# Normalising on GpSimd instead of VectorE, with a new order of the attention loop

## What is computed

```
x = x + attention(adapted_layernorm(x))      # adapter chosen by language, 16 heads of 16, one key and value head
x = x + ffn(cond2(x))                        # expert chosen per sequence, four more matrix layers
```

```
h = relu(x @ w1 + b1); adapted = h @ w2 + b2; u = x + adapted
normed = (u - mean) * rsqrt(var + LN_EPS) * gamma + beta
```

## Time and profile before

| what | us |
|---|---|
| median of 3 runs | 1109.22 (1109.03 to 1109.38) |
| the profiled execution | 1108.92 |
| its span, first to last instruction | 1107.1 |
| PE busy in the span | 1084.2 (98%) |
| DVE busy | 808.7 (73%) |
| ACT busy | 597.2 (54%) |
| POOL busy | 174.8 (16%) |

### The profile page before, as it was taken

One profiled execution on the slowest core, in us unless ns is written; L12 is line 12 of the kernel. 1 busy time (PEld: TensorE's weight loads), 2 busy tenths in 40 slices (PEclk: granted clock), 3 DMA queues, 4 the chain that ended last, 5 costly groups with the idle time before them and its releaser, 6 DMA issues.

```text
span 1107.1 us, 18530 instructions
## 1 busy us (share of the span) xinstructions
PE 1084.2 (98%) x6155; PEld 864.0 (78%) x6155; DVE 808.7 (73%) x1416; ACT 597.2 (54%) x1004; POOL 174.8 (16%) x192
## 2 busy tenths in 40 slices
PE   7899999999989999999999999999999999999998
PEld 4567777777757888888888888888888888888886
DVE  4888787878887676555687765888748787577875
ACT  2456666666655445433566555655637555455643
POOL 2122232222364434520000000000000000000000
PEclk9899999999999999999999999999999999999999
DMA  6445656567675565646054431344422444304421
GB/s 170 76 89 120 119 127 111 129 116 185 128 266 179 181 207 199 220 143 209 20 171 148 155 117 57 131 136 159 143 76 66 154 160 150 114 18 141 145 95 39
DMA packets 82256, 148.59 MB, mean 134 GB/s; under 512 B 15504, under 2 KB 42016, under 8 KB 82080
## 3 DMA queue, kind: packets, MB, share of 16 engines
q1 hardware_dynamic: 68946, 123.51, 37.4%
q10 hardware_dynamic: 13262, 24.52, 8.2%
HBM read 107.63 MB, written 30.41 MB: 125 GB/s over the span
## 4 chain that ended last, share of the span: by engine, by line
PE 94%; DVE 3%; ACT 1%; issue 1%; DMA 0%; POOL 0%; SPq 0%; DVEq 0%; ACTq 0%; POOLq 0%
PE bank L1813 37%; PE bank L1775 11%; PE bank L1530 7%; PE bank L1825 5%; PE bank L1442 5%; PE bank L1751 4%; PE bank L1745 4%; PE bank L1461 3%; PE bank L1445 3%; PE bank L1480 3%; PE bank L1378 2%; PE bank L1366 1%; PE bank L1401 1%; PE bank L1518 1%; PE bank L1500 1%; PE bank L1482 1%
## 5 line engine op out<-in xcount | busy, mean ns | idle before, releaser
L1813 PE MATMUL bank<-op_hi,w_ring 128*128 128x512 f32 x896 | 348.6, 389 | 0.0
L1813 PE MATMUL bank<-op_lo,w_ring 128*128 128x512 f32 x896 | 348.6, 389 | 0.0
L1259 DVE TENSOR_TENSOR op_lo<-x_blk,op_hi 128x512 fp32r<-128x512 f32 x288 | 193.7, 684 | 30.4 <-ACT op_hi L878 30.3
L878 ACT ACTIVATE op_hi<-x_blk 128x512 fp32r<-128x512 f32 x288 | 162.8, 620 | 73.5 <-PE bank L1813 69.3
L1813 PEld LDWEIGHTS bank<-op_lo,w_ring 128*128 128x128 f32 x896 | 168.2, 188 | 35.0
L1813 PEld LDWEIGHTS bank<-op_hi,w_ring 128*128 128x128 f32 x896 | 168.1, 188 | 35.0
L1028 DVE TENSOR_REDUCE neg_max<-bank 128x2 f32<-128x512 f32 (+1 forms) x192 | 125.1, 686 | 6.6 <-PE bank L1445 3.6
L679 ACT ACTIVATE p<-bank 128x512 f32<-128x512 f32 x192 | 107.1, 592 | 33.8 <-PE bank L1461 30.6
L902 ACT ACTIVATE x_blk<-x_blk,scales 128x512 f32<-128x512 f32 x96 | 69.3, 722 | 67.0 <-DVE x_blk L1312 28.9
L1775 PE MATMUL bank<-tile_hi,ffn_w 128*128 128x512 f32 x256 | 101.6, 397 | 0.0
L1775 PE MATMUL bank<-tile_lo,ffn_w 128*128 128x512 f32 x256 | 100.9, 394 | 0.0
(11 more groups left out here) (148 smaller groups left out, 1784.5 us busy)
## 6 DMA issues: line engine op xcount, KB each, us to landing
w_ring<-hid_scratch SPq DMA_DIRECT2D x112, 512.0 KB, 4.6
hid_scratch<-comb ACTq DMA_DIRECT2D x8, 1792.0 KB, 8.0
q_t<-q_high SPq DMA_DIRECT2D x64, 128.0 KB, 4.1
comb<-in_hid_d ACTq DMA_DIRECT2D x6, 768.0 KB, 4.7
xt<-in_x_t SPq DMA_DIRECT2D x16, 256.0 KB, 3.6
xtok<-in_x_tok SPq DMA_DIRECT2D x16, 256.0 KB
resid<-in_x_t SPq DMA_DIRECT2D x16, 256.0 KB, 3.1
x_scratch<-x SPq DMA_DIRECT2D x16, 256.0 KB, 2.6
```

The source lines that it names most:

```text
L878: nc.scalar.activation(op_hi[:, o % OP_RING, k], x_blk[:, operand_home(o), k], ACT.Copy).then_inc(s["op_hi"], 1)
L1259: nc.vector.tensor_tensor(op_lo[:, o % OP_RING, k], x_blk[:, operand_home(o), k], op_hi[:, o % OP_RING, k].bitcast(F32), ALU.subtract).the ...
L1813: last = mm(banks[first_bank + m][:, :], w, read(v[:, q % OP_RING, k, :]), start=k == 0 and v is op_hi and i not in (P2, P3), stop=k == KB ...
```

## The change

The two instructions of `normalise` move from VectorE to GpSimd, directly behind the power, and VectorE's next `add_adapted` waits until they are done with `u`. TensorE's and ScalarE's parts of the iteration stand in another order, and SP issues the residual's load ahead of the moves of the maxima.

```diff
@@ SP, iteration
                 move_high(b + 2, (slot + 2) % SLOTS)
+                load_resid(b)
                 move_maxima(b + 1, (slot + 1) % SLOTS)
                 store_x1(b - 1)
-                load_resid(b)
                 copy_ffn(b - 1)
@@ GpSimd
+            def normalise(n):
+                pool.wait_ge(s["rstd_ready"], n + 1)
+                settle(pool, "pool_settled")
+                for t in range(NT):
+                    nc.gpsimd.tensor_scalar(norm[:, t, :], u[:, t, :], moments[:, t, 0:1], rstd[:, t:t + 1],
+                                            ALU.subtract, ALU.mult).then_inc(s["norm_ready"], 1)
...
                 if front:
                     rstd_of(b + 2)
+                    normalise(b + 2)
...
             rstd_of(0)
+            normalise(0)
@@ ScalarE, iteration
-                    exponential(b, 4)
                 if front:
                     affine(b + 2)
                     norm_parts(b + 2)
+                if tail:
+                    attention_out(b - 1)
                 if softmax:
+                    exponential(b, 4)
                     exponential(b, 5)
                     exponential(b, 6)
-                if tail:
-                    attention_out(b - 1)
                 if front:
                     queries_high(b + 2)
                 if softmax:
                     exponential(b, 7)
+                    exponential(b, 8)
                 if front:
                     keys_copied(b + 2)
+                    move_low(b + 2, (slot + 2) % SLOTS)
                 if softmax:
-                    exponential(b, 8)
                     exponential(b, 9)
-                if front:
-                    move_low(b + 2, (slot + 2) % SLOTS)
-                    keys_high(b + 2, (slot + 2) % SLOTS)
+                    exponential(b, 10)
                 if maxima:
                     maxima_out(b + 1)
+                if front:
+                    keys_high(b + 2, (slot + 2) % SLOTS)
                 if softmax:
-                    exponential(b, 10)
                     exponential(b, 11)
@@ VectorE, add_adapted
+                if not is_first(n):
+                    dve.wait_ge(s["norm_ready"], NT * n)
@@ VectorE, iteration (and the same in the iterations ahead of the loop)
                 if maxima:
                     maximum(b + 1, 0)
                     maximum(b + 1, 1)
-                if front:
-                    normalise(b + 2)
                 if tail:
                     attention(b - 1, 0)
```

More of the change, by code:

```diff
@@ L1189, in _ @@
             add_adapted(0)
-            normalise(0)
             split_queries_weights()
@@ L1639, in iteration @@
                     max_scores(b + 1, ahead, 1)
+                if tail:
+                    products_transposed(b - 1, 0, front)
                 if softmax:
@@ L1642, in iteration @@
                     scores(b, slot, 1)
-                if tail:
-                    products_transposed(b - 1, 0, front)
                 if maxima:
                     max_scores(b + 1, ahead, 2)
+                    max_scores(b + 1, ahead, 3)
                 if softmax:
                     scores(b, slot, 2)
+                    scores(b, slot, 3)
                 if tail:
                     products_transposed(b - 1, 1, front)
-                if softmax:
-                    scores(b, slot, 3)
+                if front:
+                    norm_transposed(b + 2, tail)
                 if maxima:
-                    max_scores(b + 1, ahead, 3)
+                    max_scores(b + 1, ahead, 4)
+                    max_scores(b + 1, ahead, 5)
                 if softmax:
                     scores(b, slot, 4)
-                if front:
-                    norm_transposed(b + 2, tail)
-                if softmax:
-                    scores(b, slot, 5)
-                if maxima:
-                    max_scores(b + 1, ahead, 4)
-                if softmax:
-                    scores(b, slot, 6)
-                if maxima:
-                    max_scores(b + 1, ahead, 5)
                 if tail:
@@ L1670, in iteration @@
                     max_scores(b + 1, ahead, 6)
+                if softmax:
+                    scores(b, slot, 5)
+                if maxima:
                     max_scores(b + 1, ahead, 7)
@@ L1673, in iteration @@
                     project_queries(b + 2, tail)
+                if softmax:
+                    scores(b, slot, 6)
                 if maxima:
@@ L1684, in iteration @@
                     max_scores(b + 1, ahead, 10)
+                    max_scores(b + 1, ahead, 11)
                 if softmax:
                     scores(b, slot, 9)
-                if maxima:
-                    max_scores(b + 1, ahead, 11)
                 if tail:
                     project_out(b - 1, front)
+                if softmax:
+                    scores(b, slot, 10)
                 if front:
                     values_transposed(b + 2)
-                if softmax:
-                    scores(b, slot, 10)
-                    scores(b, slot, 11)
                 if maxima:
                     maxima_transposed(b + 1)
+                if softmax:
+                    scores(b, slot, 11)
             pe.wait_ge(s["warm_made"], 1)
```

7 lines of the change are left out of this document (removed).

## The result

The changed kernel takes 1122.09 us (median of 5 runs, 1118.69 to 1124.71), the kernel before 1109.22 (1108.72 to 1109.81): the ratio is 1.0112, with a 95% interval of 1.0093 to 1.0131. It is 12.9 us slower by the medians and 12.4 by the ratio, where 2.7 less had been forecast. The five runs go with the granted clock: 1118.69 at 0.998, 1120.43 at 0.995, 1122.09 and 1122.5 at 0.992, and 1124.71, the profiled one, at 0.989.

What follows compares the result with a forecast made beforehand. TensorE was taken to set the pace, held up mid-iteration by VectorE's reductions. 12 x -0.24 = -2.9 plus +0.2 at the ends made -2.7: 1106.5 us from 1109.22, range 1104.8 to 1110.5.

Steps and rivals of the forecast that it cites:

- GpSimd's price: Normalising on GpSimd: about 0.40 us per instruction, 0.80 for both, priced like casts; upper bound 3.13 for both.
- nothing is paid up to 1.1 each: Loop, norm ahead of norm_transposed: 1.4 us to spare, so GpSimd's two instructions cost nothing up to this length.
- GpSimd is slow: Rival, chance 0.10: at 1.56 each the norm is 0.9 late, 0.3 to 0.6 reach project_queries; 1111 to 1116 us.
- The ends: Outside the steady loop: first sequence +0.1 (up to +2.4), iteration 13 to 14 +0.4, iteration 14 -0.3 us.
- The relief of VectorE: Mid-iteration: without normalising, unit 5 is reduced 0.73 earlier, max_scores 7's 0.21 wait goes; 0.24 us gained per iteration.
- `max_scores` 6 and 7 0.35 to 0.39 apart: Sign that the forecast is right: these two TensorE steps, 0.60 us apart before, start this close together.
- ScalarE's end of the iteration: Before adapter_out: slack for hidden falls from 0.83 to 0.06 us, costed at 0, or 0.1 to 0.2 per iteration.
- this rival: The wait moves to ScalarE, chance 0.22: 0.1 to 0.2 us before adapter_out in each iteration; 1107.7 to 1108.9 us.
- SP and the DMAs: Residual's load ahead of the maxima's moves: query moves keep 0.6 us of slack before max_scores 0; no cost.
- the rival of the residual: Rival, chance 0.13: the residual's load delays the query moves by 1 us, making max_scores 0 0.4 late; 1111.3 us.
- The port: SBUF port shared by VectorE and GpSimd: VectorE's reductions out of PSUM do not stretch GpSimd's 0.80 us.
- The fixed piece: End of an iteration, project_out to the next adapter_in: 2.47 us, staying at about 2.5 in the new order.

Runs made afterwards that it cites:

- e8: The kernel before, with GpSimd instructions of several forms on scratch tiles added in the last phase, feeding no output: 1107.88 us in its one run.
- e1: The changed kernel with its new order on all engines, but VectorE normalises as before: 1111.16 us, ratio 1.0021 to the kernel before.
- e4: The changed kernel with more dummy matmuls while TensorE waits for the first two norms (25 for 15, 26 for 12): 1118.40 us, ratio 1.0092.
- e5: e1 with ScalarE's attention_out behind exponential 6 again in iterations 14 and 15: 1109.86 us, ratio 1.0010 to the kernel before.
- e11: The kernel before, old order, with half of the loop's normalising moved to GpSimd: 1108.53 us, ratio 0.9998.
- e10: e6 with the residual's load behind the maxima's moves again and half of the loop's normalising on GpSimd: 1106.29 us, ratio 0.9981 to the kernel before.
- e6: e5 with products_transposed 0 behind scores 0 and 1, as in the kernel before: 1111.05 us, ratio 1.0021 to the kernel before.
- e3: The changed kernel, but VectorE normalises the three sequences ahead of the loop: 1114.21 us, ratio 1.0056 to the kernel before.

## Why the prediction was wrong

**GpSimd's price.** The step that failed is "I take the casts' price, since one tensor is read, as in a cast": 0.40 each was taken, 1.22 measured (e8 and the loop). The bound named, 1.56 each, holds it. The threshold was nearly right too: the power ends 6.54 behind the iteration's start, as before, 0.21 pass, and without a wait `norm_transposed` would start at 8.82 (e1), which leaves 2.07, 1.03 each, against "nothing is paid up to 1.1 each". The pair takes 2.43, 0.36 too long, and against e1, where VectorE normalises, `project_queries` comes 0.25 later (11.77 to 12.02). The rival "GpSimd is slow" said this with 0.9 late and 0.3 to 0.6 passed on. It had the mechanism, with a chance of 0.10, but its 1111 to 1116 do not hold the 1122.09 either, as it priced the first sequence alone. Even the gap ahead of the pair was taken too small, 0.1 for 0.21. The choice was made by what an instruction reads; what it does to each element, two operations with operands per partition, was left out.

The Trainium skill ("GPSIMD Engine Reference", on engine selection) advises against elementwise work on GpSimd; that advice was right here, but the estimated 1.5 for the pair, by twice VectorE's time, fell short of the 2.43 measured, which is 3.3 times VectorE's 0.73.

**The ends.** "For the first sequence the norm is on the path: 0.73 become 0.80 here: +0.1, up to +2.4": this is the dearest error. The first upper bound was sound for one sequence (the pair takes 1.70 more), but the second and the third were not priced at all, though none has a loop's work to cover it; together 5.5. And the step has no term for the clock, which fell after TensorE's longer waits: 4.7 of the profiled execution's 9.8, and between 2 and 4 in the median (e4). From iteration 13 on the forecast was +0.4 and -0.3; measured +0.2 up to the first tile, and +2.1 behind it, of which nothing was foreseen: `attention_out` in iteration 15 (e5).

**The relief of VectorE.** "Without them unit 5 is reduced at about 201.11 - 0.73 = 200.38" supposes that the reductions "follow back to back". They do in the profile before, but only because the normalising fills the time in which VectorE would otherwise wait for `max_scores` 3 (e11: 0 gained). The order was taken for a small extra, 0.23; it is the condition. With both in place and the norm in time the gain is real: e10's 0.18 per iteration against the kernel before is three quarters of the 0.24 forecast. What is left is in the table: the new order puts 0.32 of work from ahead of `project_queries` to behind it (from its start to `project_out` 4.25 before, 4.57 in e1), the end piece is 0.09 shorter, so `project_queries` must come 0.23 earlier for nothing to be lost; e1 comes 0.19 earlier, e10 0.43. The sign named for this, "`max_scores` 6 and 7 0.35 to 0.39 apart", could not have shown it: `scores` 5 stands between the two in the new order, and they are 0.60 apart in both kernels and in e10.

**ScalarE's end of the iteration.** The slack of "0.06" was too low, and costing it at 0 was right: in an iteration of the kernel after, `project_out` starts at 218.10, `hidden` ends at 222.20 + 0.45 = 222.65, and `adapter_out` starts at 223.22:

```profile
218.10 0.63 PE L1518 MATMUL bank<-att_t,tile_hi 128*128 128x256 f32 x4
...
223.22 1.13 PE L1378 MATMUL bank<-w2c,h_t 65*128 65x256 f32 x4
...
222.20 0.45 ACT L641 ACTIVATE h_t<-bank,vec 64x256 f32<-64x256 f32 x1
```

That is 4.55 and not 4.91, with 0.57 to spare. The pieces overlap, as the text had said against this rival.

**SP and the DMAs.** No wait of TensorE for a DMA stands in the list of the kernel after, so "I take no cost" held, and the rival of the residual did not happen in it. The slack is small all the same: 0.3 in one iteration of e1, and 0.9 in all in e6. "The maxima's moves: nothing" holds only in an order in which `scores` 0 comes late.

**The port.** In the loop VectorE reduced out of PSUM while GpSimd normalised, and the instructions took 1219 to 1227 ns, where e8's took 1221 to 1223. This agrees with the Trainium skill's rule on the shared port pair ("SBUF — State Buffer", on who interferes with whom): no contention shows for the reductions. The one exception, the 1572 of the second sequence, lies ahead of the loop and beside another kind of instruction (e8).

**The fixed piece.** `project_out` to `adapter_in` was to stay at about 2.5; it went from 2.70 to 2.61 (medians), so it was fixed to 0.1.

Sum by the prediction's terms, for the profiled execution: 12 x -0.24 became 12 x +0.32 (+3.8), the first sequence's +0.1 became +9.8 over three, and the ends' +0.1 became +2.3.

What stays open: why this form costs 3.3 ns an element where the subtraction of two tensors is cheaper, and why the clock fell in some executions of the changed kernel for longer than in others, which sets 1118.69 apart from 1124.71.

## What to carry to other kernels

An instruction that moves to another engine is priced by its own form there, its operations and operands included, and where no row shows that form the end of the bounds that hurts deserves a real chance. A step that a steady loop hides has to be priced again at every place that has no such cover, the first sequences and the last ones, with the clock that an idle TensorE may lose. Relief of an engine is worth something only if what it would do next is ready: look at the instruction behind the removed one and ask when its input came.

## What the runs showed of the hardware

- On GpSimd `tensor_scalar` of 256 elements of f32 in each partition, with two operations, takes 1.22 us, and VectorE's 0.41; a subtraction of two tensors of this size takes 0.74 in the middle of four (mean 0.83), so on GpSimd the form that reads one tensor was the dearer one. Between the power and the `tensor_scalar` that waits for it lie 0.21, and between two instructions of the probe, each waiting for the one before, 0.09.
- Five instructions of GpSimd started while VectorE ran a TENSOR_TENSOR with both inputs in SBUF, and all five took longer: 1572 for 1222, 1285 for 924, 1108 for 740, 1141 and 1809 for 793. Those already under way when one began did not.
- A wait of TensorE costs more than its length where little else is to do: 1.18 in iteration 15 made 2.1 to the end of the kernel, and 5.3 of dearer norms ahead of the loop made 11.3 in the profiled execution (61.3 against the 50.0 of e3, whose clock stayed at 1.00), with a granted clock of 0.55 and 0.56 in the windows behind the waits.
- More dummy matmuls are cheap by comparison: 24 more of them took nothing that shows, and with them the first two stretches went from 40.7 to 36.1.
